# Four stages of a hybrid network on one core: set-up, semaphore upkeep and residual sums moved into the neighbouring blocks

## The reference

```python
def _layernorm(x, axis=-1, eps=1e-05):
    m = jnp.mean(x, axis=axis, keepdims=True)
    v = jnp.var(x, axis=axis, keepdims=True)
    return (x - m) / jnp.sqrt(v + eps)
...
    x = x + _L0_attn_a_ref(_layernorm(x, axis=-1), ...)   # Mamba: scan over 512 tokens
    x = x + _L0_ffn_ref(_layernorm(x, axis=-1), ...)      # 6 layers: windowed attention, feed-forward
    x = x + _L0_attn_b_ref(_layernorm(x, axis=-1), ...)   # attention that keeps the 64 largest scores
    x = x + _L0_ffn_ref(_layernorm(x, axis=-1), ...)      # the same 6 layers once more
    return x
```

## Time and profile before

| | us |
|---|---|
| median of 3 executions | 5479.3 |
| lowest, highest | 5470.51, 5499.99 |
| the profiled execution | 5468.32 |
| its span, first to last instruction | 5466.5 |

### The profile page before, as it was taken

The page is one execution under the profiler, slowest core; times in us unless marked ns, Lnnn a source line. Parts: engine busy times, 40 slices in busy tenths (PEclk is TensorE's granted clock), DMA queues, the critical chain, the costliest instruction groups (busy, mean ns, idle before and its releaser), DMA issues. The chain is left out here.

```text
span 5466.5 us, 135257 instructions
## 1 busy us (share of the span) xinstructions
PE 4736.4 (87%) x51446; PEld 3025.6 (55%) x51638; DVE 4170.8 (76%) x8694; ACT 3352.0 (61%) x7201; POOL 2732.1 (50%) x3646
## 2 busy tenths in 40 slices
PE   4775899999999999677777777667999999999997
PEld 1232666666666666434444343344666666666665
DVE  5897677777777777489898999966777777777774
ACT  2432677777777777444445444435777777777775
POOL 1221666666666666223333332325666666666663
PEclk7898999999999999888888889868999999999999
DMA  0000322222222222100000000002222222222221
GB/s 18 0 0 16 81 64 74 67 66 69 73 72 73 69 67 67 33 1 2 2 2 2 1 2 2 2 1 73 72 73 69 67 75 69 71 69 75 67 63 40
DMA packets 162489, 247.16 MB, mean 45 GB/s; under 512 B 36228, under 2 KB 56640, under 8 KB 161734
## 3 DMA queue, kind: packets, MB, share of 16 engines
q1 hardware_dynamic: 161862, 238.65, 16.7%
HBM read 36.15 MB, written 1.05 MB: 7 GB/s over the span
## 5 line engine op out<-in xcount | busy, mean ns | idle before, releaser
L942 POOL TENSOR_TENSOR f_rope<-f_rope,f_t 128x1024 f32<-128x1024 f32 x384 | 905.8, 2359 | 524.4 <-DVE f_t L856 524.4
L955 POOL TENSOR_TENSOR f_rope<-f_rope,f_rn 128x1024 f32<-128x1024 f32 x384 | 730.6, 1903 | 56.7 <-POOL f_rn L934 2.6
L861 DVE TENSOR_REDUCE f_ss<-f_sq 128x16 f32<-128x1024 f32 x384 | 459.5, 1197 | 337.2 <-ACT f_sq L723 334.8
L1808 POOL TENSOR_SCALAR tk_scores<-tk_scores,tk_m 128x408 f32<-128x408 f32 (+28 forms) x232 | 239.2, 1031 | 819.8 <-DVE tk_m L1768 647.5
L1768 DVE MAX8 tk_m<-tk_work 128x8 f32<-128x204 f32 (+38 forms) x1856 | 624.4, 385 | 31.3 <-ACT tk_neg_top L1656 30.8
L1779 DVE MATCH_REPLACE8 tk_work<-tk_m,tk_work 128x204 f32<-128x204 f32 (+51 forms) x1624 | 585.0, 370 | 0.0
L686 ACT ACTIVATE f_kT<-psum 64x512 f32<-64x512 f32 (+1 forms) x960 | 485.2, 525 | 83.4 <-PE psum L483 74.0
L723 ACT ACTIVATE f_sq<-psum 128x1024 f32<-128x1024 f32 x384 | 393.3, 1024 | 219.0 <-PE psum L492 218.5
L856 DVE TENSOR_TENSOR f_t<-psum,f_rot 128x1024 f32<-128x1024 f32 x384 | 466.3, 1214 | 0.0
L852 DVE TENSOR_TENSOR f_rope<-psum,f_rot 128x1024 f32<-128x1024 f32 x384 | 465.4, 1212 | 0.0
L878 DVE TENSOR_REDUCE f_den<-f_prob 128x16 f32<-128x1024 f32 x192 | 234.2, 1220 | 297.9 <-ACT f_prob L728 297.9
(11 more groups left out here) (237 smaller groups left out, 9536.6 us busy)
## 6 DMA issues: line engine op xcount, KB each, us to landing
f_v<-f_v_tok SPq DMA_DIRECT2D x1152, 128.0 KB, 2.4
f_v<-f_v_tok SPq DMA_DIRECT2D x768, 64.0 KB, 2.0
f_wv<-in_Wqkv SPq DMA_DIRECT2D x12, 512.0 KB, 3.9
f_wk<-in_Wqkv SPq DMA_DIRECT2D x12, 512.0 KB, 4.8
f_wq<-in_Wqkv SPq DMA_DIRECT2D x12, 512.0 KB, 4.2
f_wo<-in_Wo SPq DMA_DIRECT2D x12, 512.0 KB, 4.0
f_w<-in_W SPq DMA_DIRECT2D x12, 341.0 KB, 3.2
f_w<-in_W SPq DMA_DIRECT2D x24, 64.0 KB
```

The lines of the kernel that those rows point to most:

```text
L861: dve.tensor_reduce(ss[:, H * half:H * (half + 1)], sq[:, half, :, :], AX_X, ALU.add).then_inc(s[f"{name}_ss"], 1)
L942: pool.tensor_tensor(part, part, t2[:, half, :, :], ALU.add).then_inc(s[f"{name}_added"], 1)
L955: pool.tensor_tensor(part, part, rn[:, H * half:H * (half + 1)].unsqueeze(2).to_broadcast([P, H, DH]), ALU.mult).then_inc(s[f"{name}_norme ...
```

## The change

- `names` no longer makes blocks. All semaphores are taken once at the start, and stages that don't meet share them (tk those of Mamba, n2 those of n0, n3 those of n1, both stacks one set). Raising and clearing is written into blocks that are there anyway, as the first or last thing SP does. A last block `clear_phase` clears the 97 that are left, split over the five engines.
- `norm_phase` takes a `beside`: what SP, PE, ACT, DVE and POOL do in the same block, behind their part of the norm. The Mamba and tk weights move there. PE waits there for the last `ln_scaled` ahead of its transposes, since both use PSUM.
- The stack's clears move from DVE to POOL, beside the norm, and its first three weight transfers to SP in the same block.
- `add_phase` is gone. The sum stands at the head of DVE's list in n2 (`adds=True`) and in the store, and PE waits per sequence.
- In the load, the transfer of x is issued ahead of the first semaphore upkeep, in a small block of its own.

The work area of the norm of n1 and n3 is a piece of the stack's own tiles (`sq`, `ffn`), so those tiles are named `n_ffn` where it was `n_ln_std`. The stack's tiles have the prefix `n_` where it was `f_`. Lines of the diff:

```diff
 def names(ctx, phase, nc, *which):
-    made = {w: ctx.enter_context(nc.semaphore(f"{phase}_{w}")) for w in which}
-    with nc.Block() as block:
-        @block.sync
-        def _(sp):
-            for sem in made.values():
-                sp.sem_inc(sem, 1)
-
-    def clear():
-        with nc.Block() as block:
-            @block.sync
-            def _(sp):
-                for sem in made.values():
-                    sp.sem_clear(sem)
-
-    ctx.callback(clear)
-    return made
+    return {w: ctx.enter_context(nc.semaphore(f"{phase}_{w}")) for w in which}
+
+def first_count(eng, *groups):
+    for s in groups:
+        for sem in s.values():
+            eng.sem_inc(sem, 1)
+
+def cleared(eng, *groups):
+    for s in groups:
+        for sem in s.values():
+            eng.sem_clear(sem)
...
+def norm_phase(k, phase, beside, room, adds=False):
...
+        @block.sync
+        def _(sp):
+            beside.sync(sp)
+
+        @block.tensor
+        def _(pe):
+            ln_tensor(pe, k, s, src, 0, lambda b: pe.wait_ge(s["ln_added"], 1 + b + 1) if adds else None)
+            beside.tensor(pe)
+
+        @block.scalar
+        def _(act):
+            ln_scalar(act, k, s, dst, 0)
+            beside.scalar(act)
+
+        @block.vector
+        def _(dve):
+            if adds:
+                for b in range(B):
+                    dve.tensor_tensor(src(b), src(b), dst(b), ALU.add).then_inc(s["ln_added"], 1)
+            ln_vector(dve, k, s, src, dst, 0)
+            beside.vector(dve)
+
+        @block.gpsimd
+        def _(pool):
+            beside.gpsimd(pool)
...
+        with nc.Block() as block:
+            @block.sync
+            def _(sp):
+                sp.dma_start(x_tok[:, :, :], x_rows).then_inc(s["x_in"], 16)
+                first_count(sp, s)
...
-            sp.dma_start(x_tok[:, :, :], x_rows).then_inc(s["x_in"], 16)
...
+            first_count(sp, k.sems["n0"], k.sems["mw"], k.sems["mb"])
             sp.wait_ge(s["small_in"], 1 + 16 * 7)
...
         @block.tensor
         def _(pe):
             for b in range(B):
+                pe.wait_ge(s["added"], 1 + b + 1)
                 for t in range(TILES):
...
         @block.vector
         def _(dve):
+            for b in range(B):
+                x = k.X[:, b, PAD:ROW]
+                dve.tensor_tensor(x, x, k.XA[:, b, PAD:ROW], ALU.add).then_inc(s["added"], 1)
...
-def add_phase(k, phase):
-
+def clear_phase(k):
+
+    left = [sem for phase in ("n3", "ff", "store") for sem in k.sems[phase].values()]
     with k.nc.Block() as block:
+        @block.sync
+        def _(sp):
+            for sem in left[0::5]:
+                sp.sem_clear(sem)
...
+        class Start(Nothing):
+
+            def sync(self, sp):
+                load_v(sp, 0)
+                load_k(sp, 0)
+                load_q(sp, 0)
+
+            def gpsimd(self, pool):
+                pool.memset(kT[:, :, :, :], 0.0)
+                pool.memset(v2[:, :, :, :, :, :], 0.0).then_inc(s["zeroed"], 1)
+                pool.memset(v_tok[:, :, :, :, :], 0.0).then_inc(s["zeroed"], 1)
...
+        room = sq[:, 0, :, :].rearrange("p h e -> p (h e)").rearrange("p (b n) -> p b n", n=N), ffn[:, 0:2, :]
+        norm_phase(k, phase, Start(), room)
...
-                sp.wait_ge(s["zeroed"], 1 + 3)
-                load_v(0)
-                load_k(0)
-                load_q(0)
+                if phase == "n1":
+                    cleared(sp, k.sems["load"], k.sems["n0"], k.sems["mw"], k.sems["mb"])
+                    first_count(sp, k.sems["n2"], k.sems["tk"])
+                else:
+                    first_count(sp, k.sems["store"])
+                    cleared(sp, k.sems["n2"], k.sems["mb"])
+                sp.wait_ge(s["zeroed"], 1 + 2)
...
-                dve.memset(kT[:, :, :, :], 0.0).then_inc(s["zeroed"], 1)
-                dve.memset(v2[:, :, :, :, :, :], 0.0).then_inc(s["zeroed"], 1)
-                dve.memset(v_tok[:, :, :, :, :], 0.0).then_inc(s["zeroed"], 1)
-                dve.wait_ge(s["zeroed"], 1 + 3)
...
+            def tensor(self, pe):
+                pe.wait_ge(ln["ln_scaled"], 1 + B)
                 pe.wait_ge(load["loaded"], 1 + 16 * 9)
...
+            @block.sync
+            def _(sp):
+                first_count(sp, k.sems["n1"], k.sems["ff"])
...
+            @block.sync
+            def _(sp):
+                cleared(sp, k.sems["ff"], k.sems["n1"])
+                first_count(sp, k.sems["ff"], k.sems["n3"])
...
         load_phase(k, a)
-        norm_phase(k, "n0")
         mamba_phase(k, a)
-        norm_phase(k, "n1")
-        ffn_stack(k, a, "f0")
-        add_phase(k, "a0")
-        norm_phase(k, "n2")
+        ffn_stack(k, a, "n1")
         topk_phase(k, a)
-        norm_phase(k, "n3")
-        ffn_stack(k, a, "f1")
-        add_phase(k, "a1")
+        ffn_stack(k, a, "n3")
         store_phase(k, out)
+        clear_phase(k)
```

160 lines of the change are left out of this document (89 added, 71 removed).

## The result

The changed kernel takes 5385.4 us (median of four runs, 5380.5 to 5396.8) against 5475.7 us (four runs, 5470.5 to 5500.0): 0.983 of before, 95% interval 0.980 to 0.986. It was timed a second time among the experiments: 5379.7 against 5477.2 us, 0.981, 0.979 to 0.983. So it is 1.7 to 1.9% faster, 90 to 97 us; predicted were 5378 us and 97 us. The profiled execution has a span of 5378.7 us and a time of 5380.5 us (before: 5466.5 and 5468.3), 87.8 us less.

A forecast was written before the change was run, and what follows sets the result against it. Stacks are bound inside by PE, with DVE and ACT close behind; the gain lies in seams between stages. Seam terms sum to 93.9 us, plus 3 for the clock: 97 us, forecast 5378 us, range 5364 to 5402.

The forecast's parts named there:

- The bound: Two six-layer stacks: bound inside by PE, DVE and ACT close behind; to stay at 1745 us, wrong beyond 2 us.
- The crossing: Wherever two stages meet: entering a new block still costs 0.5 us, between bounds of 0.27 and 0.67.
- n0 to Mamba: Norm n0 to Mamba: PE's weight transposes follow the norm at once, remaining weights' work unchanged; gain 9.3 us.
- The stacks' starts: n1 to f0 and n3 to f1: first matmul 2.4 us after the norm, ACT's way next; gain 23.6 us each.
- Sums: Behind each stack: only a crossing and one of four sums remain, 1.15 us; gains 7.6 and 7.2 us.
- n2 to top-k: Norm n2 to the keys' transposes: 25 transfers covered by the norm of 16.65 us; gain 16.7 us.
- The end: Closing block: SP clears 20 semaphores instead of 3; 0.9 us lost, at most 3 us.
- The clock term: Starts of stacks, a little at Mamba and tk: shorter waits avoid the clock's fall; 3 us gain, bounds 0 and 7.
- (1): Norms: POOL's writes hold DVE until they end; 35 us less gain, time about 5413; chance 0.04.
- (2): Ten crossings: PE or ACT begins late in each new block; 10 us less gain, 5388; chance 0.09.
- (3): Norms as cover: work moved but not hidden; at twice POOL's time, gain 80 us, time 5395; chance 0.04.
- (4): Stacks: PE idling less is granted less clock there, making the kernel slower, about 5507 us; chance 0.01.

The follow-up runs named there:

- the repeated kernel: The changed kernel once more with no edit; timed again at 5379.7 against 5477.2 us, 0.981.
- fillers: Useless TensorE matmuls added in top-k: changed kernel, both places 5398.7 us, tile starts alone 5389.7; four intervals only, with table load and clears moved, 5362.1.

## Why the prediction was right, point by point

- **The bound.** Stacks unchanged: 1744.35 and 1746.92 us, off by -1.3 and +1.7 from the earlier trace rows, within the 2 us given.
- **The crossing** was taken as 0.5 us between bounds of 0.27 and 0.67. It is 0.30, 0.33 and 0.34 us in the three rows of the table in which nothing else stands, and these gained 0.2 to 0.3 us more than their term.
- **n0 to Mamba** gained 10.62 for 9.3. The norm's end and the transposes meet within 0.05 us, as said. The missing 1.3 us is the weights' work itself, taken as unchanged: from the transposes to Mamba's first matmul it was 6.20 us and is 4.88. From the first transpose to DVE's copy of `mb_w_inT` it was 3.32 us and is 2.18: the transposes now follow the norm at the high clock (a grant of 1.00 over these 2.18 us, 0.50 over the 3.32 before).
- **The stacks' starts:** 23.62 and 24.01 for 23.6. The new last wait is ACT's, as said, 2.35 us. The cover held on POOL (12.51 us busy in the norm) and on SP: the first `f_v` transfer (now `n_v`) starts 5.3 us after PE in the first stack and 7.0 us in the second, where the prediction had 8, and SP's upkeep ends 1.5 us ahead of it in the first.
- **Sums:** 7.66 and 7.55 for 7.6 and 7.2; putting them back costs 3.7 us of it, the rest is upkeep.
- **n2 to top-k:** 17.09 for 16.7; here too the set-up was through when the norm ended.
- **The end** is the term that was mis-sized: 3.09 us lost, 0.9 taken. It has two parts. From the landing of the last store to the end of the program it was 0.79 us and is 3.13, so the closing block costs 2.34 us more. The working priced SP's 20 clears and let the other engines' clears be no dearer. Their durations and first and last starts:

```profile
L357 SPq EVENT_SEMAPHORE_RANGE_CLEAR  x20: 25/25/38, 5376.2 to 5377.3; - x20
```

```profile
L362 PEldq EVENT_SEMAPHORE_RANGE_CLEAR  x20: 56/56/63, 5376.0 to 5378.3; - x20
```

```profile
L372 DVEq EVENT_SEMAPHORE_RANGE_CLEAR  x19: 54/54/60, 5375.9 to 5377.8; - x19
```

  SP needs 1.1 / 19 = 0.058 us for one, PE 2.3 / 19 = 0.12 us, DVE 1.9 / 18 = 0.11 us. An even split over five engines ends with the slowest, PE. That is inside the bounds of 0.9 and 3 us. The other 0.75 us are no clears: from the last copy out to the landing of the last store it was 2.57 us and is 3.32. The four stores are issued every 0.60 us in place of every 0.85, and from issue to landing they take (before, then after):

```profile
DMA to landing us min/median/max: 2.4/2.5/2.5
```

```profile
DMA to landing us min/median/max: 2.4/2.8/3.3
```

  In both kernels they land 0.9 us apart, so the stores that are issued sooner after one another only take longer to land. The last row but one of the table thus shows 0.75 us of gain that the last row takes back, and the prediction had no term for it.
- **The clock term**, 3 us, did not come. The first stack's four matmuls did take 1.96 us in place of 3.78, the 1.8 us hoped for; the second stack's took 3.55 us, at a grant of 0.53. In the repeated kernel they took 3.75 us, although its norm had a grant of 1.00: the clock fell in the wait of 2.34 us behind the norm (grant 0.67), where the prediction let the fall come later. Why it falls there at the second stack and not at the first is open. All stages but top-k together gave 1.0 us. And the step did not look at top-k at all, where the same clock is worth ten us: the prediction said of the stages that their insides would not move, and named the stacks alone. This was the step that failed, in its place if not in the total: 8.0 us lost in the profiled execution. The runs show that such a difference comes without the edit too (1335.7 and 1346.6 us in the kernel before); whether the edit has a part in how often it comes is open. Timed, the gains of 90 and 97 us are 6 us below and 1 us above the 95.9 us of seams and other stages.
- **Rivals.** (1) POOL holding DVE in the norms: out, by DVE's 8.55 and 8.69 us; only the small copy is held. (2) Late begins: out, 0.3 us at the crossings. DVE's first memset came 1.02 us after ACT's first instruction, and 1.03 us after it with the set-up put back; without that memset DVE begins 0.04 us after ACT (490.10 and 490.06). So the delay went with that instruction; why it begins late is open. (3) Cover too short: out as it stands, and shown at work by doubling POOL's. (4) Less clock in the stacks: out, a grant of 0.99 in both.

The total was right (97 us predicted, 90 and 97 measured) since the sum of the seams was right to 1 us; in it gains too small by 3.2 us (1.3 at Mamba, up to 0.4 at each of the other eight seams) stand against a loss too small by 2.2 us at the end. That these errors and the missing 3 us of the clock nearly cancel within the timed interval is luck; that each seam came within 0.5 us, but for Mamba's and the end, is not.

## What to carry to other kernels

Measure the stretches in which no engine works and ask of each what alone stands there; put upkeep and set-up beside a stage that leaves those engines idle, and price each seam as old distance less what is late next. At the seams such terms add up nearly exactly; the timed median can move by some us more. Follow the end of the program to the landing of its last store and not to the last copy: faster copies gave nothing there. Before a difference of a few us inside an unedited stage is given to the edit, profile the unchanged kernel again: one repeat of the kernel before, with the same stage 11 us longer, settled more than two equal profiles of the changed one.

## What the runs showed of the hardware

- The same instructions, started at the same time to 0.01 us, ran at different granted clocks in two executions (56.06 and 66.39 us for one tile). In eleven profiles without fillers the 3rd, 7th and 11th interval took 53.5 to 56.1 us with 14 to 21 us at the low clock (21 of 33), or 59.8 to 66.4 us with 34 to 48 us at it (12 of 33), and nothing between. In the one profile of each kernel with fillers in place they took 54.6 to 54.9 us, with 3.4 us at it, or 57.27 us three times, with none. Why the clock stays low longer in one execution than in another is open.
- Low clock cost nothing where VectorE was busy without a break: ten of top-k's sixteen intervals hold 225 us of it while VectorE is idle for 2.3 us or less in each. 270 us less of it in the stage, bought with fillers, made the stage no shorter.
- A clear of a semaphore costs about twice as much on PE (0.12 us) and DVE (0.11 us) as on SP (0.058 us).
- A GpSimd memset of 5.2 us held a VectorE copy of 8 x 128 bfloat16 elements to its own end, and held none of the float32 additions and multiplications beside it (four sums in 2.50 us with it and without, a norm's twelve operations in 8.69 us beside 17.35 us of memsets and 8.70 us without).
- Four stores issued every 0.60 us landed 0.9 us apart, as did those issued every 0.85 us, so the last one took 3.29 us from issue to landing in place of 2.54.
